# P times V in at most two runs of a query tile, and scores negated and scaled on their way out of the accumulators, in an attention and mixture-of-experts layer

## The reference

```
q, k, v = t @ wq[h], t @ wk[h], t @ wv[h]
score = q @ k.T * 64 ** -0.5          # causal: columns after the row are masked
attn = softmax(score, axis=-1)
out = (attn @ v) * sigmoid(gate)
pred_values += out @ wo[h]
```

## Time and profile before

| | |
|---|---|
| median of 3 runs | 773.39 us (773.01 to 776.36) |
| profiled execution, its span | 773.9 us |
| attention (four pairs) | 32 to about 575 us, one pair takes 138.8 us |
| TensorE busy with matmuls | 688.3 us, 89% |
| TensorE busy with loads of weights | 523.0 us, 68% |
| VectorE busy | 534.2 us, 69% |
| ScalarE busy | 419.2 us, 54% |

### The profile page before, as it was taken

How to read it: one execution, slowest core, us unless ns; L and a number is a source line. 1 busy time by engine, 2 the same in 40 slices (tenths; PEclk the granted TensorE clock), 3 DMA queues, 4 the chain that set the end, 5 groups by cost and what they waited for, 6 DMA issues and landing times.

```text
span 773.9 us, 17695 instructions
## 1 busy us (share of the span) xinstructions
PE 688.3 (89%) x5442; PEld 523.0 (68%) x5443; DVE 534.2 (69%) x1874; ACT 419.2 (54%) x908; POOL 105.3 (14%) x172
## 2 busy tenths in 40 slices
PE   4799999979999997999999899999958987999940
PEld 3577777747777774777777577777744556878830
DVE  4687767678777777787767888776787523556536
ACT  4766555656655557655555766554533213454445
POOL 2000000000000000000000000000021773565540
PEclk9999999998999999899999999999976996999975
DMA  8300000040000004000000694000090112222224
GB/s 188 83 2 1 2 3 1 8 107 2 1 2 2 2 1 111 3 1 1 2 2 1 145 130 4 2 2 2 1 302 25 49 52 56 65 63 64 67 73 113
DMA packets 56260, 33.64 MB, mean 43 GB/s; under 512 B 23776, under 2 KB 49520, under 8 KB 56176
## 3 DMA queue, kind: packets, MB, share of 16 engines
q1 hardware_dynamic: 53616, 27.33, 17.6%
q0 software_dynamic: 2560, 5.26, 2.0%
HBM read 14.70 MB, written 9.48 MB: 31 GB/s over the span
## 4 chain that ended last, share of the span: by engine, by line
PE 61%; issue 12%; DVE 12%; POOL 6%; ACT 4%; DMA 3%; SPq 0%; POOLq 0%; DVEq 0%; ACTq 0%
PE ps_o L1079 16%; PE ps_t L961 16%; PE ps_s L1044 9%; PE ps_s L1050 8%; POOL x_sorted L480 4%; PE ps_o L1089 3%; PE ps_s L1193 3%; DVE q_hl L674 2%; PE ps_o L1208 2%; DMA y_rows<-y_sb,row_now 1%; DVE k_l L674 1%; ACT probsT L568 1%; PE ps_s L1048 1%; DVE probs L755 1%; POOL y_rows L490 1%
## 5 line engine op out<-in xcount | busy, mean ns | idle before, releaser
L755 DVE TENSOR_SCALAR_CACHE_REDUCE probs<-ps_s 128x512 f32<-128x512 f32 (+3 forms) x320 | 192.1, 607 | 77.2 <-PE ps_s L1050 75.2
L557 ACT ACTIVATE probs<-probs,nmax 128x128 f32<-128x128 f32 (+15 forms) x128 | 154.0, 1203 | 133.5 <-DVE nmax L762 133.1
L961 PE MATMUL ps_t<-ident,probs 128*128 128x128 f32 x1104 | 181.6, 281 | 17.5 <-ACT probs L529 11.1
L961 PEld LDWEIGHTS ps_t<-ident,probs 128*128 128x128 f32 x1104 | 130.8, 142 | 64.7 <-issue 23.5
L1079 PE MATMUL ps_o<-probsT,v_sb 128*64 128x128 f32 x2176 | 154.4, 280 | 0.0
L1044 PE MATMUL ps_s<-k_h,q_hl 128*128 128x512 f32 (+3 forms) x320 | 145.2, 454 | 6.1 <-issue 5.4
L1079 PEld LDWEIGHTS ps_o<-probsT,v_sb 128*64 128x64 f32 x2176 | 115.7, 137 | 38.6 <-issue 36.1
L1050 PE MATMUL ps_s<-k_l,q_hl 128*128 128x512 f32 (+3 forms) x320 | 128.5, 402 | 0.0
L568 ACT ACTIVATE probsT<-ps_t 128x512 f32<-128x512 f32 (+3 forms) x160 | 89.6, 560 | 62.2 <-PE ps_t L961 60.8
L771 DVE COPY probsT<-ps_t 128x512 f32<-128x512 f32 (+3 forms) x160 | 91.1, 570 | 25.7 <-PE ps_t L961 25.3
L1044 PEld LDWEIGHTS ps_s<-k_h,q_hl 128*128 128x128 f32 x320 | 62.4, 195 | 19.3 <-issue 14.8
(11 more groups left out here) (150 smaller groups left out, 790.3 us busy)
## 6 DMA issues: line engine op xcount, KB each, us to landing
k_h<-k_h SPq DMA_DIRECT2D x32, 128.0 KB, 2.3
k_l<-k_l SPq DMA_DIRECT2D x32, 128.0 KB, 2.4
w_up<-in_L_ffn_W SPq DMA_DIRECT2D x2, 2048.0 KB, 12.1
xg<-x_sorted SPq DMA_DIRECT2D x48, 64.5 KB, 1.8
x_sorted<-zeros SPq DMA_DIRECT2D x12, 256.0 KB, 9.5
act_s<-y_rows SPq DMA_DIRECT2D x8, 256.0 KB, 4.9
x_acc<-in_L_attn_tokens SPq DMA_DIRECT2D x4, 256.0 KB, 3.6
out<-x_acc SPq DMA_DIRECT2D x4, 256.0 KB, 2.3
```

The lines of the kernel that those rows point to most:

```text
L557: nc.scalar.activation(probs[s % 2][h][:, 0:w], probs[s % 2][h][:, 0:w], ACT.Exp, bias=nmax[:, row], scale=SCALE, accum_out=rsum[:, row]). ...
L755: nc.vector.tensor_scalar(probs[s % 2][h][:, c * BANK:c * BANK + w], ps_s[n % RING][:, 0:w], 1.0, None, ALU.mult, ALU.max, accum_out=cmax[ ...
L961: return nc.tensor.transpose(dst, src, ident[:, :])
```

## The change

`times_v` gets units of its own, made by `pv_groups`: a tile with one or two chunks has one unit, a tile with three or four has two, cut after `n // 2` chunks. VectorE now copies the scores out of the accumulators times minus the scale, with a running minimum; the reduction over the chunks then gives the bias of the exponential directly, and the exponential takes factor -1. The wait between reduction and scaling, and the scaling, are gone.

```diff
+    def pv_groups(s):
+        n = len(chunks[s])
+        cut = n // 2 if n > 2 else 0
+        return [(a, b) for a, b in ((0, cut), (cut, n)) if b > a]
...
-            stages.append([("times_v", s - 2, 0, c, w) for c, w in chunks[s - 2]])
+            stages.append([("times_v", s - 2, 0, c, w) for c, w in pv_groups(s - 2)])
...
-                                         bias=nmax[:, row], scale=SCALE,
+                                         bias=nmax[:, row], scale=-1.0,
...
-                    elif stage == "times_v" and (c, w) == chunks[s][-1]:
+                    elif stage == "times_v" and (c, w) == pv_groups(s)[-1]:
...
-                        probs[s % 2][h][:, c * BANK:c * BANK + w], ps_s[n % RING][:, 0:w], 1.0, None,
-                        ALU.mult, ALU.max, accum_out=cmax[:, h, c:c + 1]).then_inc(freed, 1)
+                        probs[s % 2][h][:, c * BANK:c * BANK + w], ps_s[n % RING][:, 0:w], -SCALE, None,
+                        ALU.mult, ALU.min, accum_out=cmin[:, h, c:c + 1]).then_inc(freed, 1)
...
-                        link_in(nc.vector.tensor_reduce(nmax[:, row], cmax[:, h, 0:c + 1], X, ALU.max, negate=True))
-                        nc.vector.tensor_scalar(nmax[:, row], nmax[:, row], SCALE, None, ALU.mult).then_inc(row_max, 1)
+                        nc.vector.tensor_reduce(nmax[:, row], cmin[:, h, 0:c + 1], X, ALU.min).then_inc(row_max, 1)
...
-                def times_v(s, c, w):
+                def times_v(s, c, end):
...
-                    done = first[s, 1] + c + 1
+                    done = first[s, 1] + end
...
-                    for j in range(c * BT, c * BT + w // P):
+                    for j in range(c * BT, min(end * BT, t + 1)):
```

More of the change, by code:

```diff
@@ L168, in attention_moe_layer @@
         gate1 = sb("gate1", [P, NT, HEADS], f32, attn)
-        cmax = sb("cmax", [P, 2, NC], f32, attn)
+        cmin = sb("cmin", [P, 2, NC], f32, attn)
         nmax = sb("nmax", [P, 2 * NT], f32, attn)
@@ L739, in largest_logits @@
                 link(ins)
-            LINKS = 5 * NT
+            LINKS = 3 * NT
             def pair(p, units, fill_of):
```

## The result

The changed kernel takes 785.55 us (median of 4 runs, 784.02 to 787.00) against 773.88 us; the ratio is 1.0149, 95% interval 1.0122 to 1.0176. It is slower, by 11.7 us. The forecast was 788 us, slower, range 775 to 799: direction, size and range hold.

What follows compares the result with a forecast made beforehand. TensorE was taken to set the pace. Per pair, held turns +6.2 and +5.1, freed turns -1.8, fewer runs -5.6 gave +3.9, rounded to +3.7; four pairs add 15 us, giving a 788 us median, range 775 to 799.

Steps and rivals of the forecast that it cites:

- Fewer runs: P times V on TensorE: 16 fewer runs a pair at 0.35 us each save 5.6 us a pair.
- Without exception: Support for the pure-gain case: every P times V run shows its 0.17 us wait twice.
- Minimum and scale: VectorE's dropped scaling shortens each chain to the exponential by 0.19 us; counts only where a turn is held.
- (a): Six already held turns a pair, steps 5 to 12, lose a covering run: +1.04 us each, +6.2 a pair.
- (b): Six turns a pair just not held before become held when their covering run moves: together +5.1 us a pair.
- The step 8 to 9 turn: Held turn after step 8's last scores: chain 4.59 us, own work 3.05, held for 1.54 instead of 0.50.
- up to 5 us in all: VectorE late by one copy, 0.69 us, at two places a pair: +5 us at most, taken as zero.
- (c): Turns freed in step 5, step 3 and at the head of a pair: together -1.8 us a pair.
- The clock rival: New waits lower TensorE's clock in heavy steps, up to 3.4 us a pair: 802 us; above 796, chance 0.07.
- The gain rival: No new TensorE waits: 745 us, or 760 with a third of them; pure or mostly pure gain, chance 0.10.
- Two of its marks: Signs of being right: TensorE's turns wait for ScalarE's copy some 50 times, 50 to 65 us in all.
- The mark of 142.5 us for a pair: Sign of being right: a pair of heads in attention takes 142.5 us, against 138.8 before.

Runs made afterwards that it cites:

- e8: Kernel before the change with P times V on all 128 array columns, both heads added into one result; 855.43 us against 789.24 before on that chip.
- e3: Changed kernel with both runs of two-run query tiles moved earlier, ahead of the held turns; 747.92 us, ratio 0.9683 to before.
- e2: Changed kernel's minimum and dropped scaling alone, with P times V back to one run per chunk; 767.20 us, ratio 0.9912 to before.
- e1: Changed kernel's joined runs alone, with VectorE reducing, waiting and scaling as before the change; 799.75 us, ratio 1.0363 to before.
- e7: Changed kernel with its runs moved ahead of the held turns and VectorE's reduction, wait and scaling as before; 773.97 us, ratio 0.9821 to before.
- e5: Changed kernel with only the first of two runs moved earlier; 784.37 us, ratio 0.9949 to before on that chip.

## Why the prediction was right, point by point

- **Fewer runs, 0.35 us each.** The mechanism held: 0.17 us stands on both sides of runs of 16, 20, 28 or 32 loads, and e8 shows what it belongs to. "Without exception" was wrong: of the 35 runs in steps 3 to 15 of the second pair of before, eight have 0.35 to 0.37 us ahead of them, since they stand right behind a chunk of scores, and five 0.24. The size is somewhat high: e3 has 15 runs fewer in that stretch than e2, the same instructions otherwise and nearly the same waits for the two copies (3.0 against 2.6 us), and is 4.0 us shorter, which is 0.27 to 0.29 us a run. A part of the gap comes back: a turned chunk behind a run takes 0.38 us to the scores behind it instead of 0.56 (in the timeline of before, 201.16 to 201.54 against 227.61 to 228.17).
- **Minimum and scale.** Held for the changed kernel's chain (1.83 us instead of 2.01) and for e2 (-1.3 us a pair in steps 3 to 15). The other factors cost nothing, as said: VectorE's copy out of the accumulators takes 606 ns on average after and 607 before, the exponential 1204 and 1203. That VectorE's saved work is hidden everywhere else was too simple: e1 and e7 show it worth more where scores and turns stand close.
- **(a) and (b), the turns that lose their cover.** Every place is held that was forecast, and no other by ScalarE; the sizes were a little high. The step 8 to 9 turn was forecast at 4.59 us after the scores, held for 1.54; it came at 4.60, held for 1.56 with the usual 0.04. In the timeline of the changed kernel's weight loads and ScalarE, the first head of step 8 (scores at 226.40, forecast 4.45 us and held for 0.94):

```profile
230.22 0.57 ACT L574 ACTIVATE probsT<-ps_t 128x512 f32<-128x512 f32 x1
...
230.85 0.42 PEld L966 LDWEIGHTS ps_t<-ident,probs 128*128 128x128 f32 x4 [0.99 <-ACT probsT L574]
```

  and step 9 (forecast +0.33):

```profile
243.50 0.42 PEld L966 LDWEIGHTS ps_t<-ident,probs 128*128 128x128 f32 x4 [0.38 <-ACT probsT L574]
```

  4.45 us and 0.95, then 0.34. Over the second pair the six turns of (a) gained 5.5 us of hold instead of 6.2 and the six of (b) 4.4 instead of 5.1. The ones that fall short most, in (a) by 0.3 each, are in step 5 and at 249.66, held for 1.21 us where 1.46 was forecast; ahead of the latter a turn had already waited 0.44 us for VectorE.

  The sum came out by errors that go opposite ways, so a part of its closeness is luck. For steps 3 to 15 the entries give 6.2 + 5.1 for the holds, 1.2 back for those freed inside, and 5.3 saved, since one of the 16 runs (query tile 5's, in step 15) lies behind the end: +4.8 us a pair; measured +4.2. The holds on ScalarE were 1.2 too high. VectorE's copies cost 6.7 us, 1.7 a pair, which stood in the range as "up to 5 us in all" and in the sum as nothing. And the forecast took every hold at its full length, while a held turn gives a part back: a run starts 0.59 us after a held turn (237.28 to 237.87) and 0.76 after one that was not held (228.51 to 229.27). 17 turned chunks of the stretch are held instead of 7, so that is up to 1.7 us a pair; how it divides with the price of a run I did not settle.
- **(c), what comes back.** Mis-sized. Outside steps 3 to 15 the entries give 0.6 us a pair for the head of a pair and 0.35 for the run in step 15, 3.7 us in all; measured are 5.4, of which steps 0 to 2 of the four pairs give 2.8 and what follows step 15 of the last pair 1.8. Of the 2.8, 1.9 are at the head of the second pair, where the granted clock differed between the two executions. Two stretches there, of 5.5 and 6.8 us, in the changed kernel had a mean granted clock of 1.00 and 0.75; the like of the second had 0.58 before:

```profile
169.50:175.00 5.50, 2.15 (x18) 1.78 (x17) 2.03 (x6) 1.19 (x2) 0.53 (x2) 1.00 0.02 6
175.00:181.80 6.80, 6.80 (x41) 5.30 (x40) 5.18 (x24) 4.30 (x14) 0.00 (x0) 0.75 0.02 6
```

  So a part of it is no effect of the change but of where the clock fell: over the thirteen traces this passage takes 7.1 to 9.0 us, and it has 9.0 in before and 7.1 in the changed kernel. How much, two profiles don't tell.
- **The clock rival.** Did not happen. In the heavy steps TensorE was busy for 34.5 of 39 us instead of 38.8, and the clock stayed at 1.00:

```profile
217.00:256.00 39.00, 34.47 (x323) 27.22 (x323) 24.04 (x77) 20.32 (x31) 0.00 (x0) 1.00 0.01 2
```

- **The gain rival.** Wrong for this kernel; it had new waits under 5.6 us a pair, and those for ScalarE's copy alone grew by 8.9. In another order the gain comes: e3 is at 748, between the 745 and the 760 that this rival had.

The forecast was 788 against 785.5. Two of its marks held: turns waited for ScalarE 53 times ("some 50") and 52.9 us ("50 to 65"). The mark of 142.5 us for a pair missed. The first three pairs took 140.4, 140.9 and 139.0 us, on average 140.1; the 138.8 us it started from are the second pair's, and the first three of before took 136.9, 138.9 and 135.1, on average 137.0. So a pair grew by 3.1 us, where 3.7 was forecast.

## What to carry to other kernels

A piece of work that is merged or moved leaves a place, and what it did there may be to fill a wait: before joining runs to save a fixed price, ask for each place which chain ends behind it, and put the joined run ahead of the instruction that this chain holds. Here the kernel with the same 96 runs is 12 us slower than before in one order and 25 us faster in the other, the minimum included; without the minimum (e1 and e7, each against before on its chip) it is 27 us slower and 15 us faster. A wait that appears only now and then in the profile (32 times, 0.5 us each) can be the sign that an engine is balanced against a chain with nothing to spare, as it was here.

## What the runs showed of the hardware that I had not expected

- On the chip of e5 to e8 the expert part held a pause that no trace from another chip showed: ScalarE and VectorE stood still together, with a releaser that the trace puts at none of the engines. In e5, who waited for whom:

```profile
ACT sil_s L616 <- remote: 26.7, 1, 26.7
```

  TensorE then waited 22.8 us for VectorE, in all four kernels of that group alike. The cause stays open.
- The repeatability of a stretch inside an execution: steps 3 to 15 of a pair agreed to 0.1 us between chips (109.4 in both runs of the changed kernel, 100.0 in both of e3), while medians moved by 1 to 3 us. For changes under 1% such a stretch tells more than the time does.
